# Transposing q's and k's split parts with one transposing DMA per tile, with the gate and the dot product one slot later

## What is computed

```python
ada = t_emb @ w_ada + b_ada
sh_msa, sc_msa, g_msa, sh_mlp, sc_mlp, g_mlp = jnp.split(ada, 6, axis=-1)
xn = layer_norm(logmap0(x))
xm = expmap0(xn * (1 + sc_msa) + sh_msa)
q = _to_heads(plin(xm, w_q, b_q))
k = _to_heads(plin(xm, w_k, b_k))
v = _to_heads(plin(xm, w_v, b_v))
qt, kt, vt = (logmap0(q), logmap0(k), logmap0(v))
scores = jnp.einsum('bhqd,bhkd->bhqk', qt, kt) / math.sqrt(HD)
attn = jax.nn.softmax(scores, axis=-1)
out_h = expmap0(jnp.einsum('bhqk,bhkd->bhqd', attn, vt))
attn_out = plin(_from_heads(out_h), w_o, b_o)
attn_t = g_msa * logmap0(attn_out)
x = mobius_add(residual, expmap0(attn_t))
...
return mobius_add(residual, expmap0(ff_t))
```

## Time and profile before

| | |
|---|---|
| median of 3 executions | 842.89 us (840.26 to 843.83) |
| the profiled execution, its own time | 841.73 us |
| its span, first to last instruction | 839.9 us |
| mean granted TensorE clock | 0.959 of full speed |
| busy: PE, PEld, DVE, ACT, POOL | 703.7, 515.0, 673.6, 586.5, 353.3 us |
| q1 DMA queue | 49970 packets, 70.55 MB, 28.4% of 16 engines |

### The profile page before, as it was taken

The page is one execution under the profiler, slowest core; times in us unless marked ns, Lnnn a source line. Parts: engine busy times, 40 slices in busy tenths (PEclk is TensorE's granted clock), DMA queues, the critical chain, the costliest instruction groups (busy, mean ns, idle before and its releaser), DMA issues.

```text
span 839.9 us, 29703 instructions
## 1 busy us (share of the span) xinstructions
PE 703.7 (84%) x9393; PEld 515.0 (61%) x9393; DVE 673.6 (80%) x2231; ACT 586.5 (70%) x1627; POOL 353.3 (42%) x682
## 2 busy tenths in 40 slices
PE   5967999999999999999999999731868899889986
PEld 2756777777777777777777777520325555556555
DVE  3868888888888888888888888757797888888885
ACT  1125777777777777777777777633577888888874
POOL 1005555556555565555555565401232333233231
PEclk9979999999999999999999999955899999999999
DMA  9931111111111111111111110021343545455432
GB/s 324 354 86 52 51 52 51 56 56 46 50 54 56 56 43 51 56 56 52 44 54 56 55 46 27 23 66 51 88 116 98 148 137 144 126 150 151 138 102 100
DMA packets 51811, 73.99 MB, mean 88 GB/s; under 512 B 7081, under 2 KB 34609, under 8 KB 51762
## 3 DMA queue, kind: packets, MB, share of 16 engines
q1 hardware_dynamic: 49970, 70.55, 28.4%
q10 hardware_dynamic: 1792, 2.89, 0.9%
HBM read 64.24 MB, written 9.18 MB: 87 GB/s over the span
## 4 chain that ended last, share of the span: by engine, by line
PE 44%; DVE 25%; issue 14%; DMA 5%; ACT 4%; SPq 3%; DVEq 2%; POOL 2%; POOLq 0%; ACTq 0%
PE p_qkv L893 21%; PE p_oz L867 8%; DVE u L1156 7%; PE p_s L958 3%; PE p_s L883 3%; DMA mod_b<-mod_rows 3%; SPq L365 2%; DVE g_all L1191 2%; PE p_qkv L958 2%; PE p_oz L861 2%; DMA x_all<-in_x 2%; DVEq L50 2%; PE p_t L944 1%; DVE qk L1231 1%; PE p_o L972 1%
## 5 line engine op out<-in xcount | busy, mean ns | idle before, releaser
L893 PE MATMUL p_qkv<-wqkv,tT 128*128 128x256 f32 x768 | 194.3, 390 | 26.6 <-DVE u L1156 26.3
L893 PEld LDWEIGHTS p_qkv<-wqkv,tT 128*128 128x128 f32 x768 | 135.1, 192 | 57.4 <-issue 23.8
L477 POOL TENSOR_TENSOR qk<-qk 128x512 f16<-128x512 f32 x64 | 73.9, 1155 | 142.0 <-ACT qk L613 142.0
L907 PEld LDWEIGHTS p_o<-v,pT 64*64 64x64 f32 x4096 | 68.3, 136 | 36.1 <-issue 36.1
L1184 DVE TENSOR_TENSOR z<-p_oz,bo 128x256 f32<-128x256 f32 x64 | 27.1, 424 | 77.5 <-PE p_oz L867 77.3
L618 ACT ACTIVATE qkT<-p_s 128x1024 f32<-128x1024 f32 x64 | 65.5, 1023 | 31.1 <-PE p_s L850 31.1
L907 PE MATMUL p_o<-v,pT 64*64 64x17 f32 x4096 | 72.8, 209 | 12.0 <-ACT pT L663 12.0
L663 ACT ACTIVATE pT<-p_s 128x1024 f32<-128x1024 f32 x64 | 65.4, 1022 | 20.3 <-PE p_s L883 20.3
L867 PE MATMUL p_oz<-wo,oT 128*128 128x256 f32 x256 | 75.2, 418 | 0.6 <-ACT oT L623 0.5
L850 PE MATMUL p_s<-ident,qk 128*128 128x128 f16 x1024 | 67.9, 219 | 6.7 <-issue 4.5
L1222 DVE TENSOR_TENSOR qk<-u,fac 128x256 f32<-128x256 f32 x128 | 70.3, 588 | 0.1
(11 more groups left out here) (268 smaller groups left out, 1758.0 us busy)
## 6 DMA issues: line engine op xcount, KB each, us to landing
mod<-mod_rows SPq DMA_DIRECT2D x128, 128.0 KB, 2.8
x_all<-in_x SPq DMA_DIRECT2D x8, 1024.0 KB, 13.9
gate<-mod_rows SPq DMA_DIRECT2D x128, 64.0 KB, 2.5
mod<-mod_rows SPq DMA_DIRECT2D x32, 256.0 KB, 4.1
mod_b<-mod_rows SPq DMA_DIRECT2D x32, 256.0 KB, 4.1
out<-x_all SPq DMA_DIRECT2D x32, 256.0 KB, 2.2
gate<-gate_rows SPq DMA_DIRECT2D x32, 128.0 KB, 3.5
bqkv<-gate_rows SPq DMA_DIRECT2D x32, 128.0 KB, 3.8
```

Source lines behind the costliest of these rows:

```text
L477: pool.tensor_tensor(low, qk[:, :].rearrange("p (a h d) -> p a h d", a=2, d=HD), qk4[:, :, :, 0, :], ALU.subtract).then_inc(low_ready, 1)
L893: mm = pe.matmul(p_qkv[:, a * D:a * D + D], tT[:, k, c, :], wqkv[:, c, a * D:a * D + D], start=c == 0, stop=c == C - 1)
L907: mm = pe.matmul(p_o[S * e:S * e + S, col:col + VW], pT[keys, e, g, :], v[keys, k, 2 * g + e, :], start=True, stop=True, skip_group_check= ...
```

## The change

Five things change together.

1. PE's 16 transposes of `qk4`, ACT's copy to `qkT`, and the fp16 identity go. In their place SP issues one transposing DMA per tile, from `qk4` straight to `qkT`, both in SBUF, 512 KB. It waits for `again_ready` and for the previous tile's scores, and stands on SP between the slot's `mod` and `gate` DMAs. PE's `scores_wait` now waits for the DMA (`qkT_in`) instead of for ACT, and for the previous exp.
2. `qk4` gets a second buffer (in the space of `mod_b`, which is used only by the MLP pass), so that the DMA can read one while the next tile is split into the other.
3. `gate_z`, `dot_x`, ACT's square of the gated z (now its own function, `square_zg`) and POOL's `keep_stats` move one slot back (lag `L_G` = 7), and `st` gets two buffers. On DVE the order of the slot's second part becomes gate, clip, dot, bias, repeat.
4. On POOL, `token_root` stands ahead of `low_parts`.
5. The pass has 71 slots instead of 70; `bias_left` moves to `xa`.

```diff
-        L_A, L_B, L_C, L_D, L_E, L_H, L_L = 0, 1, 2, 3, 4, 5, 6
+        L_A, L_B, L_C, L_D, L_E, L_H, L_L, L_G = 0, 1, 2, 3, 4, 5, 6, 7
...
                 if on(h, off, L_H):
                     i, k = 2 * h + off - L_H, (off - L_H) % 2
+                    sp.wait_ge(again_ready, 2 * i + 2)
+                    after(sp, s_psum, i)
+                    sp.sem_inc(rows_begun, 1)
+                    sp.dma_start(qkT[:, :, :, :].rearrange("p a g n -> p (a g) n"),
+                                 qk4s[k].rearrange("p a h r d -> p (a h r d)"), transpose=True).then_inc(qkT_in, 16)
                     after(sp, zg_ready, i - 1)
...
-            def evac_qkT(i):
-                act.wait_ge(qkT_psum, i + 1)
-                after(act, s_psum, i)
-                act.activation(qkT[:, :, :, :].rearrange("p a g n -> p (a g n)").bitcast(F32), p_s[:, :], ACT.Copy).then_inc(qkT_ready, 1)
...
-            def transpose_qk(i):
-
-                pe.wait_ge(again_ready, 2 * i + 2)
-                after(pe, p_ready, i)
-                for a in range(2):
-                    for g in range(G):
-                        mm = pe.transpose(p_qkT[:, a, g, :], qk4[:, a, 2 * g:2 * g + 2, :, :].rearrange("p h r d -> p (h r d)"),
-                                          ident16[:, :])
-                mm.then_inc(qkT_psum, 1)
...
             def scores_wait(i):
 
-                pe.wait_ge(qkT_ready, i + 1)
+                pe.wait_ge(qkT_in, 16 * i + 16)
+                after(pe, p_ready, i)
...
             def slot_from_bias(h, off):
+                if on(h, off, L_G):
+                    gate_z(2 * h + off - L_G, (off - L_G) % 2, h + (off - L_G) // 2)
+                if on(h, off, L_C):
+                    clip_t(2 * h + off - L_C, (off - L_C) % 2)
+                if on(h, off, L_G):
+                    dot_x(2 * h + off - L_G, (off - L_G) % 2)
                 if on(h, off, L_L):
                     add_bo(2 * h + off - L_L)
                 if on(h, off, L_E):
-                    repeat_parts(2 * h + off - L_E)
-                if on(h, off, L_L):
-                    gate_z(2 * h + off - L_L, (off - L_L) % 2, h + (off - L_L) // 2)
-                if on(h, off, L_C):
-                    clip_t(2 * h + off - L_C, (off - L_C) % 2)
-                if on(h, off, L_L):
-                    dot_x(2 * h + off - L_L)
+                    repeat_parts(2 * h + off - L_E, (off - L_E) % 2)
```

More of the change, by code:

```diff
@@ L175, in build @@
         mods2 = (mod[:, :, :], mod_b[:, :, :])
+        qk4s = (qk4[:, :, :, :, :], mod_b[:, :, :].rearrange("p j n -> p (j n)").bitcast(F16).rearrange(
+            "p (a h r d) -> p a h r d", a=2, h=H, r=4))
         lnx2 = (lnx, t)
@@ L325, in run_tiles @@
         def run_tiles(eng, slot):
-            run_slots(eng, slot, FIRST, T, T + L_L)
+            run_slots(eng, slot, FIRST, T, T + L_G)
         def run_pairs(eng, slot):
@@ L469, in scale_v, with low_parts, keep_stats @@
                                    fac[:, 2 * H:3 * H].unsqueeze(2).broadcast_to([P, H, HD]), ALU.mult).then_inc(v_ready, 1)
-            def low_parts(i):
+            def low_parts(i, k):
                 pool.wait_ge(high_ready, i + 1)
                 pool.wait_ge(qk_ready, 2 * i + 2)
-                after(pool, qkT_psum, i)
-                low = bass.AP(qk4[:, :, :, :, :].tensor, 2 * HD, [[8 * H * HD, P], [4 * H * HD - HD, 2], [4 * HD, H], [1, HD]])
-                pool.tensor_tensor(low, qk[:, :].rearrange("p (a h d) -> p a h d", a=2, d=HD), qk4[:, :, :, 0, :],
+                after(pool, qkT_in, 16 * (i - 1))
+                big = qk4s[k]
+                low = bass.AP(big.tensor, big.offset + 2 * HD, [[8 * H * HD, P], [4 * H * HD - HD, 2], [4 * HD, H], [1, HD]])
+                pool.tensor_tensor(low, qk[:, :].rearrange("p (a h d) -> p a h d", a=2, d=HD), big[:, :, :, 0, :],
                                    ALU.subtract).then_inc(low_ready, 1)
-            def keep_stats(i):
+            def keep_stats(i, k):
                 pool.wait_ge(z_squared, i + 1)
@@ L605, in _, with high_parts @@
                            p_oz[0:3, D:2 * D].rearrange("p (b n) -> p b n", n=P), ACT.Copy, scale=2.0).then_inc(ffw_made, 1)
-            def high_parts(i):
+            def high_parts(i, k):
                 act.wait_ge(qk_ready, 2 * i + 2)
[L610 to L613, removed]
-            def evac_qkT(i):
-                act.wait_ge(qkT_psum, i + 1)
-                after(act, s_psum, i)
-                act.activation(qkT[:, :, :, :].rearrange("p a g n -> p (a g n)").bitcast(F32), p_s[:, :], ACT.Copy).then_inc(qkT_ready, 1)
+                after(act, qkT_in, 16 * (i - 1))
+                act.activation(qk4s[k][:, :, :, 0, :], qk[:, :].rearrange("p (a h d) -> p a h d", a=2, d=HD), ACT.Copy).then_inc(high_ready, 1)
             def evac_oT(i):
@@ L648, in inverse_norms, with square_z, square_zg @@
                 act.activation(y0[:, :], lnh[:, :], ACT.Exp, scale=-0.5).then_inc(y0_ready, 1)
-            def square_z(i):
+            def square_z(i, k):
                 act.wait_ge(z_ready, i + 1)
-                after(act, stats_kept, i)
+                after(act, stats_kept, i - 1)
                 after(act, z_squared, i)
-                act.activation(junk[:, 1, :], z[:, :], ACT.Square, accum_out=st[:, 0:1]).then_inc(z_squared, 1)
+                act.activation(junk[:, 1, :], z[:, :], ACT.Square, accum_out=st[:, k, 0:1]).then_inc(z_squared, 1)
+            def square_zg(i, k):
                 act.wait_ge(zg_ready, i + 1)
@@ L1223, in scale_qk, with repeat_parts @@
                                       fac[:, a * H:a * H + H].unsqueeze(2).broadcast_to([P, H, HD]), ALU.mult).then_inc(qk_ready, 1)
-            def repeat_parts(i):
+            def repeat_parts(i, k):
                 dve.wait_ge(high_ready, i + 1)
                 dve.wait_ge(low_ready, i + 1)
-                after(dve, qkT_psum, i)
-                q4, k4 = (qk4[:, a, :, :, :].rearrange("p h (y z) d -> p h y z d", y=2) for a in range(2))
+                after(dve, qkT_in, 16 * (i - 1))
+                q4, k4 = (qk4s[k][:, a, :, :, :].rearrange("p h (y z) d -> p h y z d", y=2) for a in range(2))
                 dve.tensor_copy(q4[:, :, :, 1, :], q4[:, :, :, 0, :]).then_inc(again_ready, 1)
```

43 lines of the change are left out of this document (19 added, 24 removed).

## The result

The changed kernel takes **933.6 us** (median of 4 executions, 929.5 to 937.6) against 843.4 us before (840.3 to 844.5): the ratio is **1.108, 95% interval 1.102 to 1.114**. Forecast were 910 us and slower. The measured time lies in the stated range; the sum gave a step of 67 us, and the step was 90 us.

The account below looks back on a forecast made before the run. A loop of waits, 7.50 us per attention slot, bounds the kernel. With a 4.6 us DMA landing and SP's queue the slot becomes 8.55, +67 us over 64 slots: 910 us; range 829 to 1065, 857 to 939 for the forecast itself.

Parts of the forecast that it names:

- the sum: Attention-pass slot P = (12.5 + 4.6) / 2 = 8.55 us, 1.05 more per slot, 64 slots: +67 us.
- PE's and ScalarE's savings cost at nothing: Attention pass: PE loses 67.9 us and ACT 65.5 us of busy time, both beside the loop, so no gain.
- x, the landing: Time from the transposing DMA's issue to its landing, taken as 4.6 us.
- The low end, 2.95: Lowest landing estimate: 2.2 us for 256 KB from SBUF plus 0.75 for another 256 KB at 350 GB/s.
- Rival 1: Transposing DMA moved in small pieces, 0.063 us per packet, landing over 5.5 us; high end 1240 us; chance 0.19.
- Rival 2: Transposing DMA's 16 blocks go one after another, landing after 21 us, time over 1900 us; chance 0.04.
- SP's queue holds the DMA back: Four DMAs ahead on SP, the first awaiting the gate operation, delay the transposing DMA to 3.1 us after gate end.
- The two-slot loop: Late landing delays the next slot's gate and thus SP's next transposing DMA: P = (12.5 + x) / 2, x the landing time.
- gate end at 6.17: On DVE, gate operation ends 6.17 us after u: `limit` at 2.07, 3.65 to the last sum's end, gate 0.45.
- Without any wait for the new DMA the slot would be 7.3 us: Attention slot with the later gate and no DMA wait, set by modulation rows: 7.3 us, gain 13 us.
- The loop through the modulation rows: SP issues gate and mod after the gate operation; the next slot's `modulate` needs that `mod`: 7.4 us, taken as 7.3.
- Rival 3: Landing under 2.5 us or shorter SP issues, PE not held, slot 7.3 us, 829 us; chance 0.14.

Follow-up runs that it names:

- the run with fillers: Changed kernel plus 16 small constant products on PE while it waits for the transposing DMA: 930.2 us.
- The run that restores 0.42 us: Changed kernel with 16 filler products on PE, and GpSimd's `low_parts` also held until the gate operation is done: 913.7 us.
- the order with the early gate: Changed kernel with gate, clip and dot product back after z and the copies (lag 6), transposing DMA kept: 909.1 us.
- the order with the projection first: Changed kernel, gate DMAs a slot later, last q/k/v third and projection before the DMA wait, norms before exp: 841.6 us; with 16 filler products 912.3.

## Why the prediction was right in sign and 24 us short

- **PE's and ScalarE's savings cost at nothing: right.** PE's busy time in the stretch fell from 91 to 78 us of 100 and ScalarE's from 76 to 52, and none of it shortened the slot.
- **x, the landing: right to 0.2 us.** I took 4.6 us from two `mod` DMAs of 256 KB; it was 4.4. That the rows of another kind of transfer came so near is partly luck. The low end, 2.95, had left out that even a plain DMA from SBUF to SBUF takes 3.5. Rival 1 guessed the cut rightly (pieces of 256 bytes), but each costs about 19 ns and not 63, which was a mean over mixed packets and no price of a small one, so the case that it priced at 1240 us did not come. Rival 2, blocks one after another, is out: 16 blocks land in 4.4 us, though "VectorE: DVE Perf Modes", The three transpose paths, of the Trainium skill, has 1309 ns for a single one.
- **SP's queue holds the DMA back: right.** The two-slot loop gave 0.7 us after u for the issue; in the 41 slots at full clock from 85 to 560 us it was 0.76 on average. With the hold removed the kernel took 871.9 us, where x alone gives 0.26 + 4.4 + 3.26 = 7.9 us a slot.
- **The step that failed is a term of that sum: "gate end at 6.17", with 0.45 us for the gate operation.** It took 0.8 us in the changed kernel and 1.0 with the clock held, because its new place lies beside GpSimd's `low_parts`. With 1.03 us and the measured x, P = (12.5 + 0.6 + 4.4) / 2 = 8.75, and the run with fillers had 8.89. The run that restores 0.42 us took 913.7.
- **That 913.7 is near the forecast is in part luck.** With x = 4.4 the sum gives 8.45 us and 903 us, so about 10 us came from elsewhere: the wait for the held subtraction in that run, and two readings that missed in opposite directions (means of the changed kernel): `limit` at 1.5 us after u instead of 2.07, and 4.2 us instead of 3.65 from there to the gate. In the changed kernel itself the gate's mean of 0.81 us explains some 12 us of the miss by the same halving; the rest is the fall of the clock, as far as the runs show, and terms that no run takes apart.
- **The clock: not foreseen, and small.** It fell to 0.91 in the attention pass, where I had expected 1.00. Holding it gave 3 us net here. In the order with the early gate every second slot was 1.4 us longer at the lower clock, but no run holds it there.
- **"Without any wait for the new DMA the slot would be 7.3 us": wrong.** The loop through the modulation rows was found, but undersized. It takes 8.0 us: the second mod lands about 3.1 us after its issue, not 2.8, and from `modulate` to the gate's end it is 2.6 us, not 2.3. Rival 3 would have been a loss even with a landing of nothing. That error was hidden, as the DMA's loop was longer.

## What to carry to other kernels

When a transfer replaces work on engines that are off the path, nothing is gained, and if the slot's loop passes through the transfer its latency is the cost; look first at whether it does, and then at what stands ahead of it in the issuing queue. An operation that is moved one stage back moves everything that waits for its buffer, DMAs of other tensors included: here the queue entries behind the gate, not the gate, made the loss, and issuing them one slot later turned the same move from +3.5% into -1.3%. Before an operation is put into VectorE's idle time, check what GpSimd does at that moment. And a clock that falls in some slots is not priced by comparing those slots with the others, since the next slot can give the time back.

## What the runs showed of the hardware

- A transposing DMA of 128 x 2048 fp16 from SBUF to SBUF lands after 4.4 us, half of it after 3.2, and a plain one of the full size after 3.5. Its issue occupies SP's queue for 1.7 to 3.2 us, against 0.5. It goes as 2048 packets of 256 bytes.
- A VectorE operation of two SBUF inputs (128 x 256 f32) took 0.42 us alone and 1.02 us on average (0.7 and 1.35 in turn) where it met a GpSimd `tensor_tensor` of 1.16 us.
- PE's granted clock fell to its lower level for some slots after PE had waited for the transposing DMA (1.35 of 4 us busy from 416 to 420 us of the changed kernel, then a clock of 0.57 to 424 us), and 16 small products in that wait kept it at the upper one. In the order with the projection first they did not.
